# Order of the first group's work, and the places of the block-input split and of the second weights' pieces in a group's slot

## The reference, cut to what matters

```
x: (2048, 39, 16) fp32      W0: (1, 39*39, 128)      W1: (1, 39*128, 128)
x1 = einsum('bid,bjd,ijh->bhd', x,  x, W0.reshape(39, 39, 128))
x2 = einsum('bid,bjd,ijh->bhd', x, x1, W1.reshape(39, 128, 128))
y  = sum over d of concatenate([x1, x2], axis=1)          # (2048, 256)
```

## Time and profile before

| | |
|---|---|
| Time, median of 3 runs (lowest to highest) | 581.03 us (580.76 to 582.3) |
| Time of the profiled execution | 579.92 us |
| Its span, first to last instruction | 578.1 us |
| Mean granted TensorE clock | 0.994 of full |
| Busy share: PE, POOL, DVE, ACT | 95%, 83%, 82%, 81% |
| DMA | 163.78 MB, mean 283 GB/s |
| Chain that ended last, by engine | PE 71%, ACT 10%, DMA 6%, issue 5%, POOL 4% |

### The profile page before, as it was taken

The page is one execution under the profiler, slowest core; times in us unless marked ns, Lnnn a source line. Parts: engine busy times, 40 slices in busy tenths (PEclk is TensorE's granted clock), DMA queues, the critical chain, the costliest instruction groups (busy, mean ns, idle before and its releaser), DMA issues.

```text
span 578.1 us, 10856 instructions
## 1 busy us (share of the span) xinstructions
PE 550.1 (95%) x3186; PEld 483.1 (84%) x3186; DVE 472.1 (82%) x816; ACT 470.0 (81%) x983; POOL 480.9 (83%) x407
## 2 busy tenths in 40 slices
PE   5788788999999999999999999999999999999998
PEld 3476677878888888988988998898889889889988
DVE  4688888888888898888889888888988888888740
ACT  4698888889888888888888888888888888888740
POOL 6998899899989888889988888898888899888800
PEclk9799999999999999999999999999999999999999
DMA  8999999999899989999999989999999989988210
GB/s 318 331 352 317 326 312 304 306 305 295 267 306 332 307 298 290 279 324 287 288 301 312 303 268 305 315 296 293 313 285 281 325 292 300 295 304 285 52 52 10
DMA packets 66489, 163.78 MB, mean 283 GB/s; under 512 B 10112, under 2 KB 18816, under 8 KB 66432
## 3 DMA queue, kind: packets, MB, share of 16 engines
q1 hardware_dynamic: 66432, 163.09, 88.0%
HBM read 139.98 MB, written 2.10 MB: 246 GB/s over the span
## 4 chain that ended last, share of the span: by engine, by line
PE 71%; ACT 10%; DMA 6%; issue 5%; POOL 4%; DVE 2%; SPq 1%; ACTq 0%; DVEq 0%; POOLq 0%
PE acc L397 12%; PE acc L399 11%; PE acc L398 11%; PE fin L448 6%; PE fin L449 6%; PE fin L450 6%; DMA outs<-w_dram 5%; PE pg L433 5%; PE pg L431 5%; PE pg L432 5%; ACT fh L510 4%; PE turn L409 4%; PE acc L392 2%; POOL fl L761 2%; ACT gh L552 1%
## 5 line engine op out<-in xcount | busy, mean ns | idle before, releaser
L761 POOL TENSOR_TENSOR fl<-fs,fh 128x512 fp32r<-128x512 f32 x192 | 249.7, 1304 | 42.8 <-ACT fh L510 40.1
L397 PE MATMUL acc<-fh,w0h 128*128 128x512 f32 x384 | 160.3, 417 | 15.3 <-ACT x L533 10.1
L756 POOL TENSOR_TENSOR fs<-xr,xs 128x512 f32<-128x512 f32 x128 | 163.0, 1295 | 0.9 <-DMA xr<-xb_dram 0.8
L647 DVE TENSOR_TENSOR fp<-xl,xr 128x512 f32<-128x512 f32 x192 | 133.5, 697 | 31.4 <-ACT xl L517 18.4
L399 PE MATMUL acc<-fl,w0h 128*128 128x512 f32 x384 | 151.9, 395 | 0.0
L398 PE MATMUL acc<-fh,w0l 128*128 128x512 f32 x384 | 151.5, 395 | 0.0
L651 DVE TENSOR_TENSOR fl<-fp,fh 128x512 fp32r<-128x512 f32 x192 | 131.9, 687 | 23.1 <-ACT fh L510 18.2
L510 ACT ACTIVATE fh<-fp 128x512 fp32r<-128x512 f32 x192 | 114.5, 596 | 36.3 <-PE acc L399 30.6
L666 DVE TENSOR_TENSOR gl<-pg,gh 128x320 fp32r<-128x320 f32 x252 | 117.0, 486 | 25.8 <-ACT gh L552 20.6
L510 ACT ACTIVATE fh<-fs 128x512 fp32r<-128x512 f32 x192 | 121.4, 632 | 10.8 <-PE acc L399 8.6
L552 ACT ACTIVATE gh<-pg 128x320 fp32r<-128x320 f32 x252 | 105.5, 439 | 18.4 <-PE pg L433 17.6
(11 more groups left out here) (67 smaller groups left out, 724.0 us busy)
## 6 DMA issues: line engine op xcount, KB each, us to landing
xr<-xb_dram SPq DMA_DIRECT2D x192, 512.0 KB, 5.7
xbd<-xdhl SPq DMA_DIRECT2D x256, 80.0 KB, 4.0
xs<-xa_dram SPq DMA_DIRECT2D x64, 256.0 KB, 4.1
xdr<-xd_dram SPq DMA_DIRECT2D x64, 160.0 KB, 3.9
xp<-xpairs_dram SPq DMA_DIRECT2D x32, 256.0 KB, 4.3
outs<-w_dram SPq DMA_DIRECT2D x9, 256.0 KB, 6.6
out_dram<-outs SPq DMA_DIRECT2D x7, 256.0 KB, 5.8
fs<-w0a_dram SPq DMA_DIRECT2D x1, 256.0 KB, 4.8
```

Of the source, the lines that this page charges most:

```text
L397: nc.tensor.matmul(acc[:, :], w0h[:, t, :], fh[:, t, :], start=t == 0, stop=False)
L647: nc.vector.tensor_tensor(f_at(t), xl[:, :], xr[:, gi % 2, t, :], ALU.mult).then_inc(prod_dve, 1)
L756: nc.gpsimd.tensor_tensor(f_at(t), xr[:, gi % 2, t, :], xs[:, gi % 2, :], ALU.mult)\
L761: nc.gpsimd.tensor_tensor(fl[:, t, :], f_at(t), fh[:, t, :], ALU.subtract).then_inc(low_pool, 1)
```

## The change

- In every slot from 1 on, `xd_split` moves: on ACT from behind `turned_high` to ahead of `high(g+1, 0)`, on POOL from behind `low(g, 5)` and `low(g+1, 1)` to ahead of both. In slot 0 ACT keeps the old place.
- In the slots with W1, `w1_high_part` moves on ACT from behind `xd_split` to right behind `high(g+1, 0)`, `w1_low_part` on POOL ahead of `low(g, 5)`, and on DVE ahead of product 3. SP issues `w1_load` right behind `load_xd`, ahead of the two `load_right`.
- Around group 0: `w0a_raw[0]` moves to the tile 4 place of group 1's right factors, so that POOL's product 4 need not wait for W0. ACT takes `high(0, 1)` before the first W0 part, tile 3 before tile 4 (`HIGH_FIRST`), and `high(0, 5)` and `left_out(0, 1)` before the copy for `w0q`. DVE makes product 0 of group 1 before it finishes `w0q`. SP issues `load_right(0, 1, 2)` after two parts of W0 instead of three. On POOL products 1 and 4 of group 1 move into the list for group 0, and the two `xd_split` stand behind `low(1, 1)` and `low(1, 4)`.
- `WARM` goes from 10 to 9.

```diff
--- before.py
+++ after.py
@@ -42,6 +42,7 @@
 SBUF_F = {5: 0, 1: 1, 4: 2}
 ORDER = (*range(NT), FULL, FULL)
 HIGH = (0, 1, 2, 4, 3, 5)
+HIGH_FIRST = (0, 1, 2, 3, 4, 5)
 NU = NT // 2
 W0_PART = 4
 W0_FROM = {0: 1, W0_PART: 2, FULL: 3}
@@ -49,7 +50,7 @@
 EARLY = 1
 PIECES = -(-M // NW)
 W1_SLOT = 6
-WARM = 10
+WARM = 9
 
 
 def rows_of(s, late):
@@ -149,7 +150,7 @@
         xl = ps("xl", [P, GC])
         fp = ps("fp", [P, 2, GC])
         outs_as_w = outs[:, :, :].rearrange("p a b -> p (a b)").rearrange("p (t h) -> p t h", h=H)
-        w0a_raw = [fs[:, SBUF_F[4], :].rearrange("p (t h) -> p t h", h=H),
+        w0a_raw = [xr[:, 1, NT - 2, :].rearrange("p (t h) -> p t h", h=H),
                    xr[:, 1, NT - 1, :].rearrange("p (t h) -> p t h", h=H)]
         w0b_raw = [outs_as_w, x1[:, :].rearrange("p (t h) -> p t h", h=H)]
 
@@ -222,7 +223,7 @@
                 eng.wait_ge(prod_dve, nth_of(DVE_PROD, g, t))
 
         def wait_high(eng, g, t):
-            eng.wait_ge(high_done, nth_of(HIGH, g, t))
+            eng.wait_ge(high_done, nth_of(HIGH if g else HIGH_FIRST, g, t))
 
         def wait_low(eng, g, t):
             if t in POOL_LOW:
@@ -331,14 +332,14 @@
                         sp.wait_ge(xd_low, g + 2)
                     if more2:
                         load_xd(g + 2)
+                    if (first or second) and 0 <= g + 1 - W1_SLOT < PIECES:
+                        w1_load(g + 1 - W1_SLOT)
                     if more3:
                         wait_product(sp, g + 1, 3)
                         load_right(j, gi + 3, 1)
                     if more3:
                         wait_product(sp, g + 1, 5)
                         load_right(j, gi + 3, 2)
-                    if (first or second) and 0 <= g + 1 - W1_SLOT < PIECES:
-                        w1_load(g + 1 - W1_SLOT)
                     if gi == 2 and not (first or second):
                         send(j - 2)
 
@@ -356,7 +357,8 @@
             load_xd(0)
             load_right(0, 1, 1)
             sp.dma_start(idn[:, :], ident).then_inc(ident_in, 16)
-            sp.wait_ge(w0_ready, 3)
+            sp.wait_ge(w0_ready, 2)
+            sp.wait_ge(w0_high, 3)
             load_right(0, 1, 2)
             wait_product(sp, 0, 0)
             wait_product(sp, 0, 4)
@@ -574,8 +576,12 @@
                     if prev2:
                         g_high_part(j, gi - 2, 0, was_odd, j - 1 if gi == 1 else None)
                         g_high_part(j, gi - 2, 1, was_odd, None)
+                    if more and g:
+                        xd_split(j, gi + 1, False)
                     if more:
                         high(g + 1, 0, False)
+                    if (first or second) and 0 <= g - W1_SLOT < PIECES:
+                        w1_high_part(g - W1_SLOT)
                     if first and gi == 0:
                         x1_out(0, True)
                     if gi % 2 == 0 and prev:
@@ -590,10 +596,8 @@
                         high(g + 1, 2, False)
                     if prev:
                         turned_high(g - 1)
-                    if more:
-                        xd_split(j, gi + 1, first and gi == 0)
-                    if (first or second) and 0 <= g - W1_SLOT < PIECES:
-                        w1_high_part(g - W1_SLOT)
+                    if first and gi == 0:
+                        xd_split(0, 1, True)
                     if more:
                         high(g + 1, 4, False)
                         high(g + 1, 3, False)
@@ -604,20 +608,20 @@
 
             left_out(0, 0, True)
             high(0, 0, True)
+            high(0, 1, True)
             act.wait_ge(w0_sum, 1)
             nc.scalar.activation(w0h[:, 0:W0_PART, :], w0a_raw[0], COPY).then_inc(w0_high, 1)
-            high(0, 1, True)
             high(0, 2, True)
+            high(0, 3, True)
             high(0, 4, True)
-            high(0, 3, True)
             act.wait_ge(w0_sum, 2)
             nc.scalar.activation(w0h[:, W0_PART:NT, :], w0a_raw[1][:, 0:NT - W0_PART, :], COPY).then_inc(w0_high, 1)
             nc.scalar.activation(x1th[:, 0:2, :], w0a_raw[1][:, NT - W0_PART:W0_PART, :], COPY).then_inc(w0_high, 1)
+            high(0, 5, True)
+            left_out(0, 1, False)
             nc.scalar.activation(w0q[:, :, :], w0b_raw[1][:, NT - W0_PART:W0_PART, :], COPY).then_inc(w0_high, 1)
-            high(0, 5, True)
             squares(0, True)
             xd_split(0, 0, True)
-            left_out(0, 1, False)
             chunk(0, True, False, False, False)
             chunk(1, False, True, False, True)
             for j in range(2, NCH - 1):
@@ -687,6 +691,9 @@
                     if more:
                         product(j, gi + 1, 2, False)
                         low(g + 1, 0)
+                    if 0 <= g - W1_SLOT < PIECES:
+                        w1_low_part(g - W1_SLOT)
+                    if more:
                         product(j, gi + 1, 3, False)
                     if gi % 2 == 0 and prev:
                         squares_low(CP * j + gi // 2)
@@ -700,8 +707,6 @@
                         low(g + 1, 2)
                     if prev:
                         turned_low(g - 1)
-                    if 0 <= g - W1_SLOT < PIECES:
-                        w1_low_part(g - W1_SLOT)
                     if more:
                         low(g + 1, 3)
 
@@ -725,6 +730,7 @@
             dve.wait_ge(w0_high, 2)
             nc.vector.tensor_tensor(w0l[:, W0_PART:NT, :], two, w0h[:, W0_PART:NT, :], ALU.subtract)\
               .then_inc(w0_ready, 1)
+            product(0, 1, 0, False)
             dve.wait_ge(w0_high, 4)
             last_lo = w0b_raw[1][:, NT - W0_PART:W0_PART, :]
             nc.vector.tensor_tensor(last_lo, last_lo, w0q[:, :, :], ALU.subtract).then_inc(w0_sum, 1)
@@ -784,17 +790,18 @@
                 for gi in range(CB):
                     g = CB * j + gi
                     more = not (last and gi == CB - 1)
-                    if more:
+                    if more and g:
                         product(j, gi + 1, 1, False)
                         product(j, gi + 1, 4, False)
-                    if g:
-                        low(g, 5)
-                    if more:
-                        low(g + 1, 1)
+                    if more and g:
                         xd_split(g + 1, gi + 1)
                     if (first or second) and 0 <= g - W1_SLOT < PIECES:
                         w1_low_part(g - W1_SLOT)
-                    if more:
+                    if g:
+                        low(g, 5)
+                    if more and g:
+                        low(g + 1, 1)
+                    if more and g:
                         low(g + 1, 4)
                     if gi == (CB - 1 if second else 5) and not first:
                         first_out(j - 1, not odd)
@@ -803,11 +810,15 @@
               .then_inc(xbd_zero, 1)
             product(0, 0, 1, True)
             low(0, 1)
-            pool.wait_ge(w0_ready, 1)
             product(0, 0, 4, True)
             low(0, 4)
+            product(0, 1, 1, False)
             low(0, 5)
+            product(0, 1, 4, False)
+            low(1, 1)
             xd_split(0, 0)
+            low(1, 4)
+            xd_split(1, 1)
             chunk(0, True, False, False, False)
             chunk(1, False, True, False, True)
             for j in range(2, NCH - 1):
```

## The result

The changed kernel takes 605.35 us (median of 6 runs, 601.95 to 608.16) against 581.66 us for the kernel before in the same comparison. The ratio is 1.041, with a 95% interval from 1.036 to 1.046: slower by about 24 us. The sign was as forecast; 588.7 us and the range up to 594 were not. An execution more than 1.5% above the fastest of its kernel is left out of the ratios.

The account below looks back on a forecast made before the run. PE was taken as the bound from 152.00 us on, the raw block input as the thread before. Slot 1 +5.3, slots 2 to 5 +1.9, clock +0.5, the rest 0: +7.7 on 581.03 gives 588.7 us; 8-in-10 range 581.5 to 594.

Parts of the forecast that it names:

- Group 0: Start of the kernel up to `x1_out(0)`: to come at about 17.6 us instead of 17.83.
- The later `w0q`: In group 0: later by about 0.8 us, still before tile 5, costing nothing; at most 0.8 if that cover failed.
- Slot 1: Later block-input loads delay tile 5 of group 1; `x1_out(1)` at 35.8 instead of 30.48, +5.3 us, bounds +4.1 to +7.3.
- the third load: In slot 1: third `load_xd` issued at 27.2 instead of 24.02, landing 4.0 us later at 31.2.
- the clock: PE idle longer before 34 us, so matmuls behind the stall run at half rate: +0.5 us, between 0 and +1.5.
- Slots 2 to 5: Work queues behind the block input's landing; 8.45 us a slot, +1.9 us, bounds +0.1 to +4.0.
- The round trip: Slots 2 to 5: two slots take 12.5 us plus the landing; at about 4.4 both fit, 8.45 a slot.
- Slots 6 to 15: The 6.4 us of W1 waits go, block-input waits replace them; 8.97 a slot, term 0, bounds -5.8 to +2.5.
- Slots 16 to 63: Steady slots: 8.0 us each by the round trip, under PE's 8.39, so term 0; upper bound +14.
- The third rival: The split stalls steady slots too: landings of 4.9 in a third of them, +5 us, 593 and more; chance 0.12.
- The estimate after the Trainium skill: Block-input landing as fixed 2.0 us plus bytes over 436 GB/s: 2.4 us for 160 KB, time 586.5 us; not adopted.

Follow-up runs that it names:

- e3: The changed kernel with GpSimd's first split (group 0) straight behind the low part of tile 5, ahead of product 4 and `low(1, 1)`; 601.02 us.
- e1: The changed kernel with the block-input split back in its old place on ScalarE and GpSimd in every slot from 1 on; 590.3 us.
- e11: The changed kernel with the edits of e1 and e3 together; 588.25 us.
- e12: The kernel of e11 with the copies and subtractions on W1 back in their old places, the W1 load still early; 580.49 us.
- e2: The kernel before with only the block-input split moved ahead on ScalarE and GpSimd, slots from 1 on; 594.97 us, ratio 1.023.
- e5: The kernel before with only the W1 load issued right behind the block-input load, ahead of the two right-factor loads; 576.69 us, ratio 0.995.
- e6: The changed kernel with only GpSimd's split back in its old place, ScalarE's still early; 605.73 us in one execution.
- e10: The changed kernel with SyncE issuing the block-input load ahead of the four block copies and the pair load; 606.37 us.

## Why the prediction was wrong, step by step

- *Group 0*, forecast 17.6, measured 18.64. The later `w0q` was said to lie under tile 5's low part. Both came late: POOL's low part ended at 16.69, not 16.3, and tile 5 began at 16.84 (16.11 before). The squares tile then had to wait until 17.84 (16.87 before) for DVE, whose two W0 instructions took 0.77 and 1.37 us instead of the 0.41 and 0.42 of before, and it ran at 1.2 GHz, 0.77 us for 0.40. That the sum is near the 0.8 us named as the price without that cover is luck, and group 0 also varies by as much between traces of the same order.
- *Slot 1*, forecast +5.3 at its end (35.8 for 30.48, the 0.2 us of group 0 in it), measured +9.4 (39.88), 8.6 of it in the slot. The mechanism was right: e3 and e1 each take 4 us away, both together 6.0. The term was mis-sized at the third load: 4.0 us to landing taken, 6.1 measured. The chain up to its issue took 9.65 us from `x1_out(0)`, as forecast (9.6). The 4.0 us were read from the kernel before, which has the same transfers ahead of this load. Why they did not hold stays open. Behind the landing, from tile 5 to `x1_out(1)`, it was 2.7 us instead of 1.75, with PE at 0.50; I had booked the clock in slots 2 to 5 alone.
- *Slots 2 to 5*, forecast +1.9 and +0.5 for the clock, measured +2.6. The size is luck. The round trip with a landing of 4.4 us is not what happened: the loads issued there landed in 2.5 to 3.7 us, median 3.1, which in my own sum gives no loss at all. The loss is in slots 4 and 5, by one stop of 1.99 us for the low part of x1 and the slower clock behind it, the same thread as in the steady slots. In e1, e11 and e12, with the split back, slots 4 and 5 take what they took before (8.1 and 7.8); these kernels lose their 2 us in slot 2 instead (10.44 in e12, 8.12 before), which the changed kernel does not (8.36). With the split forward on the kernel before, in e2, slots 4 and 5 are long again (11.24 and 9.99).
- *Slots 6 to 15*, forecast 0, measured +0.4. ACT's waits for W1 went from 6.4 to 1.3 us and 4.2 us of waits for the block input came, as I had said. But the balance hides larger parts that I did not give. The early load alone gains 4.9 (e5). The early W1 work costs 6.5 where the split is in its old place (e11 against e12), mainly by waits for W1 itself and on POOL. With the split early too the stretch is 2.1 shorter again (90.02 against 92.15 in e1), for a reason that was not looked at.
- *Slots 16 to 63*, forecast 0, measured +11.6. This is the step that failed: "the earlier place costs nothing there". It failed in two ways. I followed one thread, from the split over ACT's list to `x1_out`, and found cover there; PE in fact stops for the low part of the turned x1, which DVE makes at the end of an unbroken row. In the kernel before that low part ended at 310.52 and PE's G began at 311.19. These 0.67 us are the same in all even slots but the first of a chunk (0.3), and 1.5 in the odd ones; a G that does wait begins 0.06 us behind the low part. So there were 0.6 us of cover at a place that I had not looked at. And I set the median landing (3.5) against the cover, when each landing over the cover is lost for good and none under it gives anything back. The third rival had the stretch, and put 5 us and a chance of 0.12 on it.
- The estimate after the Trainium skill (page "DMA: Bandwidth & Descriptors", section "Anatomy of one DMA — SWDGE (gpsimd) path"), 2.4 us for 160 KB, is near one landing here, 2.2 us with the queue idle before it, and far from the 6.1 with other transfers under way. The fit has no term for those, and its path is that of DMAs issued by GpSimd, while SyncE issues these.

Open: why the third load took 6.1 us, and why slot 2 is 2 us long in e1, e6 and e10 to e12 and not in the changed kernel. A kernel in which the early split waits for no transfer at all was not tried; it needs more buffers for the raw and the split block input.

## What to carry to other kernels

Before moving an instruction ahead on an in-order engine, list all that queues behind it on every engine downstream, and take the cover from the thread with the least, not from the one you know. When its operand comes by DMA, compare the cover with the spread of landings, not their median, and do not carry a landing over to a chain that has been shifted. Move the transfer earlier, and leave its consumer late: that half alone was the gain here.

## What the runs showed of the hardware

The same 160 KB load landed after 2.2 us with the queue idle before it (DMA share 0.01 from 19 to 22 us) and after 6.1 us with 2.4 MB issued in the 6 us before it, in one trace, 6 us apart. In the kernel before, 2.4 MB issued in the 6.4 us before it went with a landing of 4.0 us, so the bytes issued ahead do not settle the time.

Some VectorE instructions are long beside GpSimd. The two of 128x256 elements on W0 ran in each of the 14 kernels. In ten cases a GpSimd instruction was well under way as one of them began: it took 0.52 to 1.37 us and ended 0.28 us after the GpSimd instruction, every time. The other 18 took 0.41 to 0.43. The subtraction of the squares took 0.69 us where no GpSimd instruction was running as it began; where one was well under way, it ended 0.55 us after that one, and took up to 1.77 us. A GpSimd instruction that began meanwhile was long in turn, 1.42 to 1.77 us for 1.28 in the changed kernel's steady slots. That the one waits for the other to end is read from these times; it was not tried apart.
